# Keys and queries of the second attention rotated as even and odd halves of four heads, then moved to each head's rows by DMA inside SBUF

## The reference, cut to what matters

```
q_in, k_in, v_in = layer_norm(query), layer_norm(key), layer_norm(value)
q = _rope((q_in @ Wq + bq) as heads);  k = _rope((k_in @ Wk + bk) as heads);  v = v_in @ Wv + bv
scores = q k^T / sqrt(64), masked by length;  attn = softmax(scores);  out = (attn v) @ Wo + bo

def _rope(x):                      # freqs repeated, so that dimensions 2i and 2i+1 share an angle
    x1, x2 = (x[..., 0::2], x[..., 1::2])
    rot = jnp.stack([-x2, x1], axis=-1).reshape(x.shape)
    return x * cos + rot * sin
```

## Time and profile before

| what | value |
|---|---|
| median of 3 runs | 2965.04 us (2964.72 to 2965.73) |
| the profiled execution | 2966.61 us, its span 2964.4 us |
| busy in the span | PE 90%, DVE 68%, ACT 49%, POOL 46% |
| mean granted TensorE clock | 0.945 of full speed |

### The profile page before, as it was taken

How to read it: one execution, slowest core, us unless ns; L and a number is a source line. 1 busy time by engine, 2 the same in 40 slices (tenths; PEclk the granted TensorE clock), 3 DMA queues, 4 the chain that set the end, 5 groups by cost and what they waited for, 6 DMA issues and landing times. The chain is left out here.

```text
span 2964.4 us, 82177 instructions
## 1 busy us (share of the span) xinstructions
PE 2670.8 (90%) x32664; PEld 1595.9 (54%) x32664; DVE 2012.9 (68%) x6356; ACT 1449.6 (49%) x2239; POOL 1369.2 (46%) x1219
## 2 busy tenths in 40 slices
PE   4679999999989758999999999999999999996498
PEld 3423333333355735666666666666666666664365
DVE  3468888888845757676667766766667667662755
ACT  2347777777735025545546445455454454442222
POOL 2000000000000037887878878878878788785200
PEclk8789999999978859999999999999999999998799
DMA  5421111111000030000000000000000000001000
GB/s 155 146 86 27 22 25 22 25 27 22 19 20 11 1 97 7 7 25 6 18 13 7 18 13 8 24 7 18 13 7 18 13 7 7 7 2 50 0 0 14
DMA packets 109775, 75.29 MB, mean 25 GB/s; under 512 B 43923, under 2 KB 101723, under 8 KB 108896
## 3 DMA queue, kind: packets, MB, share of 16 engines
q1 hardware_dynamic: 109408, 70.16, 8.5%
HBM read 56.70 MB, written 13.43 MB: 24 GB/s over the span
## 5 line engine op out<-in xcount | busy, mean ns | idle before, releaser
L1449 ACT ACTIVATE a_probs<-psS 128x1024 f32<-128x1024 f32 (+1 forms) x448 | 431.7, 964 | 631.2 <-PE psS L1330 627.1
L634 ACT ACTIVATE a_probs<-psS 128x1024 f32<-128x1024 f32 (+2 forms) x512 | 443.6, 866 | 207.3 <-PE psS L575 207.1
L1766 POOL TENSOR_TENSOR a_acc<-a_acc,a_probs 128x512 f32<-128x512 f32 x320 | 407.4, 1273 | 225.7 <-ACT a_probs L1449 222.8
L1353 PE MATMUL psX<-a_probs,a_values 128*64 128x256 f32 x3328 | 446.5, 386 | 1.4
L661 DVE CUSTOM_DVE_ANT_0 a_junk<-psT,a_mask 128x384 f16<-128x384 f32 (+1 forms) x683 | 378.3, 573 | 61.4 <-PE psT L551 41.6
L1768 POOL TENSOR_TENSOR a_acc<-a_acc,a_probs 128x512 f32<-128x512 f32 x320 | 407.1, 1272 | 25.1
L938 POOL MEMSET r_ones<- 128x128 f16 x1 | 0.2, 206 | 839.8 <-POOLq L697 839.8
L1610 DVE CUSTOM_DVE_ANT_0 a_junk<-psT,a_mask 128x400 f16<-128x400 f32 (+1 forms) x514 | 282.6, 573 | 154.0 <-PE psS L1305 86.2
L1610 DVE CUSTOM_DVE_ANT_0 a_junk<-psS,a_mask 128x400 f16<-128x400 f32 (+1 forms) x510 | 280.7, 573 | 148.7 <-PE psT L1305 83.9
L1353 PEld LDWEIGHTS psX<-a_probs,a_values 128*64 128x64 f32 x3328 | 224.7, 137 | 105.4 <-issue 24.2
L1740 POOL TENSOR_TENSOR a_klo<-a_kt,a_khi 128x400 f16<-128x400 f32 (+1 forms) x256 | 242.9, 949 | 21.3 <-ACT a_khi L1501 21.3
(11 more groups left out here) (337 smaller groups left out, 5616.4 us busy)
## 6 DMA issues: line engine op xcount, KB each, us to landing
a_kd<-p_kst SPq DMA_DIRECT2D x24, 416.0 KB, 3.1
a_wq<-in_wq SPq DMA_DIRECT2D x64, 128.0 KB, 2.0
a_keys<-a_kd SPq DMA_DIRECT2D x96, 75.0 KB
p_ctx<-in_ctx SPq DMA_DIRECT2D x8, 768.0 KB
a_ctx<-in_ctx SPq DMA_DIRECT2D x8, 768.0 KB
a_queries<-a_lowest SPq DMA_DIRECT2D x256, 0.5 KB, 2.0
p_mask_raw<-in_mask_t SPq DMA_DIRECT2D x16, 224.0 KB, 4.4
a_queries<-a_qd SPq DMA_DIRECT2D x64, 52.0 KB
```

Source lines behind the costliest of these rows:

```text
L634: nc.scalar.activation(dst, src, ACT.Exp).then_inc(exp_done, 1)
L1353: ins = nc.tensor.matmul(w.sums[n % 2][64 * hd:64 * hd + 64, 0:T], w.values[:, n % 2, c, 64 * hd:64 * hd + 64], w.probs[:, k % RING1, 2 * ...
L1449: nc.scalar.activation(dst, src, ACT.Exp).then_inc(exp_done, 1)
L1766: nc.gpsimd.tensor_tensor(acc, acc, src[:, :, 0, :], ALU.add).then_inc(sum_step, 1)
```

## The change

Keys and queries are made for four heads at once (a quad: two pairs), as two products: all even dimensions of the four heads (4 x 32 rows), and all odd ones. Weights, biases and tables are reordered on the way in for that; wk1x goes, with its load and its split. A quarter is still two pieces of the ring, now with 128-column matmuls, and is made every second iteration instead of every one: in even iterations quarters 0 and 1, in odd ones quarters 2 and 3, always in slots 0 and 3. DVE rotates by four products and two sums: even x cos - odd x sin, odd x cos + even x sin. ACT and POOL split the sum into parts of both halves in one instruction, two slots later. Then rows 32 at a time must go to the rows of their head: SP issues four DMAs from SBUF to SBUF for each move, in all 8 to 16 a pair. Aheads now stand four ring pieces together in slots 1, 2, 4 and 5, values in slots 1, 2, 5 and 6, the query in slot 6 of even iterations. The first iteration is -4 instead of -3. The core of the diff:

```diff
-AHEAD1 = [2, 2, 1, 1, 1, 1, 0]
+AHEAD1 = [0, 2, 2, 0, 2, 2, 0]
 KEPT1 = 4
 RING1 = 5
-VALUES1 = {2: (0, 1), 4: (2, 3)}
-ITERATIONS1 = range(-3, PAIRS1 + 1)
+QUADS1 = PAIRS1 // 2
+VALUES1 = {1: (0,), 2: (1,), 5: (2,), 6: (3,)}
+KEY_SLOTS1 = {0: 0, 3: 1}
+SPLIT_AFTER1 = 2
+HALF1 = 804
+ITERATIONS1 = range(-4, PAIRS1 + 1)
...
+def quad_in(it):
+
+    m = (it + 4) // 2
+    return m if it >= -4 and m < QUADS1 else None
+
+
+def quarter_in(it, sl):
+
+    return it % 2 * 2 + KEY_SLOTS1[sl] if sl in KEY_SLOTS1 and quad_in(it) is not None else None
+
+
+def split_in(it, sl):
+
+    return quarter_in(it, sl - SPLIT_AFTER1)
+
+
+def query_in(it):
+
+    return quad_in(it) if it % 2 == 0 else None
+
+
+def query_split_in(it):
+
+    return quad_in(it) if it % 2 == 1 else None
...
+            def blocks(n):
+                for hd in range(2):
+                    for part in range(2):
+                        p0, r0 = 32 * (2 * (n % 2) + hd), 64 * hd + 32 * part
+                        yield slice(p0, p0 + 32), slice(r0, r0 + 32), part
+
+            def give_queries(n):
+                sp.wait_ge(q_lo, n // 2 + 1)
+                for src, dst, part in blocks(n):
+                    sp.dma_start(w.queries[dst, n % KEPT1, :, :],
+                                 w.made_queries[src, :, part, :]).then_inc(keys_in[n % KEPT1][0], 16)
+
+            def give_keys(n, js):
+                sp.wait_ge(k_lo, 4 * (n // 2) + js[-1] + 1)
+                made, at0 = made_at(js[0])
+                o, width = QUARTER_AT[js[0]], sum(QUARTER[j] for j in js)
+                for src, dst, part in blocks(n):
+                    sp.dma_start(w.keys[dst, n % KEPT1, :, o:o + width],
+                                 made[src, :, part, at0:at0 + width]).then_inc(keys_in[n % KEPT1][part_of(n, js[0])], 16)
...
+                    if sl == 0 and is_pair(it + 3):
+                        if it >= 1:
+                            sp.wait_ge(b_full, SLOTS1 * it)
+                        give_queries(it + 3)
+                        give_keys(it + 3, (0, 1))
+                        if it % 2 == 0:
+                            give_keys(it + 3, (2, 3))
+                    if it % 2 == 1 and sl in (2, 5) and is_pair(it + 3):
+                        give_keys(it + 3, (2 if sl == 2 else 3,))
...
+            def key(q, j, part):
+                b, o, width = q // 4, QUARTER_AT[j], QUARTER[j]
+                out = piece(("key", q, j, part))
+                pe.wait_ge(w_lo, 2)
                 pe.wait_ge(c_lo, 4 * b + 4)
-                o, width = QUARTER_AT[j], QUARTER[j]
                 hi, lo = w.chi[:, b % 2, o:o + width], w.clo[:, b % 2, o:o + width]
+                c0 = (2 * (q % 4) + part) * P
                 for i, (split, moving) in enumerate(((0, hi), (1, hi), (0, lo))):
-                    for hd in range(2):
-                        c0 = p * P + 64 * hd
-                        ins = nc.tensor.matmul(out[64 * hd:64 * hd + 64, 0:width], w.wk[:, part, split, c0:c0 + 64], moving,
-                                               start=(i == 0), stop=(i == 2), skip_group_check=True)
+                    ins = nc.tensor.matmul(out[:, 0:width], w.wk[:, split, c0:c0 + P], moving, start=(i == 0), stop=(i == 2))
...
+            def key_hi(q, j):
+                for part in range(2):
+                    act.wait_ge(near_free[bank_of(("key", q, j, part))], uses_of(("key", q, j, part)))
+                if q > 0:
+                    wait_given(act, 2 * q - 2, j)
+                    wait_given(act, 2 * q - 1, j)
+                made, o = made_at(j)
+                width = QUARTER[j]
+                nc.scalar.copy(made[:, 0, :, o:o + width], w.kt[:, j % 2, :, 0:width]).then_inc(k_hi, 1)
...
-            def rotate(n, j):
-                o, width = QUARTER_AT[j], QUARTER[j]
-                straight, crossed = (take(("key", n, j, part)) for part in range(2))
-                bias = w.bk[:, n % PER_BATCH, :]
-                done = 4 * n + j
-                if n == 0 and j == 0:
-                    dve.wait_ge(mask_ready, 16 * 12)
+            def rotate(q, j):
+                width, done = QUARTER[j], 4 * q + j
+                cols = slice(QUARTER_AT[j], QUARTER_AT[j] + width)
+                names = [("key", q, j, part) for part in range(2)]
+                even, odd = (take(name)[:, 0:width] for name in names)
+                bias = w.bk[:, q % 4, :]
+                if done == 0:
+                    dve.wait_ge(tables, 32)
+                if done >= 1:
+                    last = ("key", (done - 1) // 4, (done - 1) % 4, 1)
+                    dve.wait_ge(near_free[bank_of(last)], uses_of(last))
                 if done >= 2:
-                    before = ("key", (done - 2) // 4, (done - 2) % 4, 0)
-                    dve.wait_ge(near_free[bank_of(before)], uses_of(before))
-                nc.vector.scalar_tensor_tensor(w.crossed[:, j % 2, 0:width], crossed[:, 0:width], bias[:, 1:2],
-                                               w.sin[:, o:o + width], ALU.add, ALU.mult
-                                               ).then_inc(near_free[bank_of(("key", n, j, 1))], 1)
-                nc.vector.scalar_tensor_tensor(straight[:, 0:width], straight[:, 0:width], bias[:, 0:1],
-                                               w.cos[:, o:o + width], ALU.add, ALU.mult).then_inc(k_step, 1)
-                if n > 0:
-                    dve.wait_ge(k_lo, 4 * (n - 1) + j + 1)
-                dve.wait_ge(near_free[bank_of(("key", n, j, 1))], uses_of(("key", n, j, 1)))
+                    dve.wait_ge(k_lo, done - 1)
+                for part, src in enumerate((even, odd)):
+                    nc.vector.scalar_tensor_tensor(w.swung[:, part, 0:width], src, bias[:, part:part + 1], w.sin[:, cols],
+                                                   ALU.add, ALU.mult)
+                for part, src in enumerate((even, odd)):
+                    ins = nc.vector.scalar_tensor_tensor(src, src, bias[:, part:part + 1], w.cos[:, cols], ALU.add, ALU.mult)
+                ins.then_inc(k_step, 1)
                 dve.wait_ge(k_step, done + 1)
-                nc.vector.tensor_tensor(w.kt[:, o:o + width], straight[:, 0:width], w.crossed[:, j % 2, 0:width],
-                                        ALU.add).then_inc(near_free[bank_of(("key", n, j, 0))], 1)
-
-            def rotate_query(n):
-                name = ("query", n)
+                nc.vector.tensor_tensor(w.kt[:, j % 2, 0, 0:width], even, w.swung[:, 1, 0:width],
+                                        ALU.subtract).then_inc(near_free[bank_of(names[0])], 1)
+                nc.vector.tensor_tensor(w.kt[:, j % 2, 1, 0:width], odd, w.swung[:, 0, 0:width],
+                                        ALU.add).then_inc(near_free[bank_of(names[1])], 1)
...
-                    if is_pair(it + 3) and sl == 3:
-                        rotate_query(it + 3)
-                    if is_pair(it + 3) and sl >= 3:
-                        rotate(it + 3, sl - 3)
+                    if query_in(it) is not None and sl == 6:
+                        rotate_query(query_in(it))
+                    if quarter_in(it, sl) is not None:
+                        rotate(quad_in(it), quarter_in(it, sl))
...
+            def key_lo(q, j):
+                pool.wait_ge(k_hi, 4 * q + j + 1)
+                made, o = made_at(j)
+                width = QUARTER[j]
+                nc.gpsimd.tensor_tensor(made[:, 1, :, o:o + width], w.kt[:, j % 2, :, 0:width],
+                                        made[:, 0, :, o:o + width], ALU.subtract).then_inc(k_lo, 1)```

The order of instructions, first PE in slots 3 and 4. The names: a1_wk, a1_chi, a1_clo are key weights and context parts, a1_khi/a1_qhi (before) and a1_keys/a1_queries (now) the split keys and queries, psS, psT0 and psT1 PSUM banks. Before (slot 3's query, key quarter, weigh and totals; the first product of a piece waits for the ring's near_free):

```order
L1294 MATMUL psT1<-xT,a1_wq 64x256 [waits a1_wq_ready1,a1_near_free3]
L1294 MATMUL psT1<-xT,a1_wq 64x256 x3
L1269 MATMUL psS<-a1_chi,a1_wk 64x400 [waits a1_c_lo,a1_w_lo,a1_near_free0]
L1269 MATMUL psS<-a1_chi,a1_wk 64x400 x3
L1269 MATMUL psS<-a1_clo,a1_wk 64x400 x2
L1269 MATMUL psS<-a1_chi,a1_wk 64x400 [waits a1_c_lo,a1_w_lo,a1_near_free1]
```

More of the change, by code:

```diff
@@ L1074, in count_pieces @@
                 order += [("value", it + 1, v) for v in VALUES1.get(sl, ())]
-            if is_pair(it + 3) and sl == 3:
-                order.append(("query", it + 3))
-            if is_pair(it + 3) and sl >= 3:
-                order += [("key", it + 3, sl - 3, part) for part in range(2)]
+            if query_in(it) is not None and sl == 6:
+                order.append(("query", query_in(it)))
+            if quarter_in(it, sl) is not None:
+                order += [("key", quad_in(it), quarter_in(it, sl), part) for part in range(2)]
             if is_pair(it + 1) and sl == 1:
@@ L1214, in _ @@
             load_masks(1)
```

(23 more changed lines are left out.)

216 lines of the change are left out of this document (105 added, 111 removed).

## The result

| | time, us | ratio to before |
|---|---|---|
| before, 4 runs | 2964.88 (2961.43 to 2965.73) | |
| after, 4 runs | 3137.49 (3135.99 to 3141.50) | 1.058, interval 1.057 to 1.059 |
| forecast | 3056 (2955 to 3130) | 1.031 |

The change makes the kernel slower, as forecast, but by 173 us instead of 90, and the time lies above the range.

The account below looks back on a forecast made before the run. PE's own order of work was taken to bound the second attention; 20.2 us of work plus 5.0 of waits made 25.2 against 23.72 us, 1.5 longer, times 60 iterations 90 us on 2966.6: 3056 us, range 2955 to 3130.

Parts of the forecast that it names:

- The removed work: PE's path in the second attention: fewer key quarters, query products and aheads, from 23.72 to 20.2 us an iteration.
- The added waits: PE waiting for banks behind aheads: 2.38 us in slots 0 and 1, 0.56 slot 2, 1.5 slots 3 and 4, 0.56 slot 5.
- between the two: Slot 1's waits, in pieces within 2.5 us, placed between a 1.92 us wait with a clock fall and 1.61 without.
- The clock falls in most iterations: Rival, chance 0.13: PE's clock falls, 1.5 us lost an iteration, up to 90 us more, 3146 us.
- its own signs of being wrong: Period of 20 to 22 us without PE or POOL gaps, ACT waiting for a move, or stage clock clearly below 0.99.
- The sentence of the Trainium skill: Rule asking only for no idle gap longer than any of these waits; by it the clock never falls, time 3056 us.
- The moves: SP's issues at 0.38 us each, costed at nothing; late moves were a rival, chance 0.07, 3086 to 3116 us.
- If each issue took twice as long: Case for SP's moves: ACT would be 4 us late every second iteration, a good part meeting the exponential's slack.
- the cover it named: For late moves: the exponential's own slack, which would meet a good part of ACT's 4 us delay.
- Prologue and tail: Four half-filled iterations instead of three at the start, one fewer with keys at the end; set against each other within 5 us.

Follow-up runs that it names:

- e5_split: e4_order with the moves of keys and queries split and reissued in another order, and aheads taken through the quarters in order; 2872.6 us, 0.969 of before.
- e7_cosine: The changed kernel with a rotation of two operations, cosine products only, sine products and sums left out (result differs); 2988.9 us, 1.007 of before.
- e4_order: The changed kernel with only the ring's pieces reordered: aheads of slots 0 and 3 before the keys, none in slots 1 and 4; 3020.9 us, 1.019 of before.
- e1_fill: The changed kernel with matmuls of some aheads in slots 1 and 4 repeated into the same bank, so PE works where it waited; 3119.4 us, 1.052 of before.
- e2_still: The changed kernel without its moves of keys and queries, which are set to zero once; 3117.2 us, 1.052 of before.
- e6_values: e5_split with the fourth value group in slot 5 instead of slot 6; 2885.4 us, 0.973 of before.

## Why the prediction failed

- **The removed work** was put about 0.5 us an iteration too high: 25.26 less the waits below leaves 20.7 us, where 20.2 was said. In e5_split, with the aheads in another order, the mean period is (21.33 + 22.69) / 2 = 22.0 us, with waits of 0.5 to 0.9 us still in it in front of slot 6's aheads.
- **The added waits** were right in place and releaser, and near in size. Slot 1 waits 1781.36 - 1778.76 - 0.44 = 2.16 (said 2.38), slots 2 and 5 0.56 and 0.57 (0.56), slot 4 1.25 (1.5): 4.5 in all, where 5.0 was said. The fall-free iteration is 25.26 (25.2), but so close only by luck, since the two misses of 0.5 cancel. e7_cosine and e4_order show from both sides what makes the waits: shorten the rotation, or take the aheads away from behind it, and the waits go.
- **The step that failed is the clock.** The prediction put the waits "between the two" rows, 1.92 with a fall and 1.61 without, costed the falls at nothing in the sum, and gave "The clock falls in most iterations" 0.13 and 3146 us. That rival is what happened: 46 falls in 63 iterations, 39 more than before, and at 1.6 us each they are 62 of the 81 us that the forecast lacked. A granted clock clearly below 0.99 was among its own signs of being wrong, and so was ACT waiting for a move. A single wait was compared with single waits, where the three pieces of slot 1 leave PE 0.91 us of work in 2.50. The sentence of the Trainium skill that was weighed against it, in TensorE: Matmul & The Clock Gate, section Why this matters for your kernels, would have kept the clock up; the 18 falls in plain iterations, behind waits of at most 1.3 us apiece, are against it. The same page's section A second HAM failure mode: psum-queue depth-cycling describes this kernel better: short idle stretches between groups of matmuls that cycle through PSUM banks let the clock swing between its levels. It was not weighed, and e1_fill agrees with it: with the idle stretches filled, the plain iterations keep the clock.
- **The moves** were mis-sized: an issue takes 0.63 us instead of the 0.38 that was read from moves out of DRAM. The text had seen this end ("If each issue took twice as long"), and the cover it named held: 10 us in the stage. But the cover was the waits themselves, as e4_order and e7_cosine show.
- **Prologue and tail** were set against each other within 5 us; they cost 11 and give back 3, the 2 of the last iterations and 0.9 behind the stage. Nine of the 11 are moves that nothing hides before the stage (e2_still).

What stays open: why the clock falls behind a wait in one iteration and keeps up behind the same wait in another, and why the moved value group of e6_values lengthens the waits of iterations 2 and 4. Whether the new order of the ring would have made the kernel before faster as well was not tried, so how much of e5_split's 3.1% belongs to the quads is not shown.

## What to carry to other kernels

Work that is taken off an engine gives nothing if it stood in front of a wait: ask first which instruction queues behind the longest chain on the other engine, and move that one: here the order of the ring's pieces alone (e4_order) gave back 117 us, and with the moves apart (e5_split) 265. When a change spreads several waits close together on TensorE, price the clock for the whole stretch, not for the longest wait in it. A cost that is hidden behind a wait comes back when the wait is removed, so remove the two together.

## What the runs showed of the hardware

- An issue of a DMA from SBUF to SBUF takes SP 0.62 to 0.63 us for 100, 50 and 32 KB, and for half of these; in the same kernel four moves from DRAM of 75 to 100 KB take 1.52, 0.38 each, and one of 128 KB takes 0.59. What sets the cost, no run shows beyond its not following the bytes.
- A DVE sum of 128x400 with one operand in PSUM takes 0.57 us, with POOL at work beside it (at most 0.58) or not; with both in SBUF it takes 0.58 without POOL's work and beside it 1.00 in the median, up to 1.64.
- TensorE fell to half clock behind three waits that left it 0.91 us of work in 2.50, the longest of them 1.30, and in other iterations it kept the clock behind the same three; in the kernel before it had not fallen behind one of 1.61.
